# The running row maximum of a graph-attention layer, stored grouped by remainder of four

## The reference, cut to what matters

```
scores = einsum('hbnd,hbdm->hbnm', f_self, f_other)
masked = a * scores ; masked = where(masked >= 0, masked, 0.2 * masked) / 4
attn = softmax(masked - 1e9 * (a == 0), axis=-1) ; zero where a == 0
out = relu(attn @ feats + bias)
```

## Time and profile before

| | |
|---|---|
| median of 3 runs | 1647.0 us (1645.42 to 1648.21) |
| span of the profiled execution, first to last instruction | 1639.9 us |
| time of the runs outside that span (median less span) | 7.1 us |
| busy: TensorE / VectorE / ScalarE / GpSimd | 87% / 81% / 76% / 66% |
| mean granted TensorE clock | 0.947 |

### The profile page before, as it was taken

The page is one execution under the profiler, slowest core; times in us unless marked ns, Lnnn a source line. Parts: engine busy times, 40 slices in busy tenths (PEclk is TensorE's granted clock), DMA queues, the critical chain, the costliest instruction groups (busy, mean ns, idle before and its releaser), DMA issues.

```text
span 1639.9 us, 22202 instructions
## 1 busy us (share of the span) xinstructions
PE 1428.8 (87%) x7728; PEld 705.3 (43%) x7728; DVE 1329.8 (81%) x1657; ACT 1243.4 (76%) x1475; POOL 1077.2 (66%) x575
## 2 busy tenths in 40 slices
PE   5897879998998899998889998988899889899766
PEld 3443434444444444444444444444444444345323
DVE  2887878888887888888888788888888788988865
ACT  2697878787887879877787778878788787887731
POOL 3367767766777666677676667777677766767422
PEclk9999999999999999999999999999999999999867
DMA  6523251313423053121513234131342304100000
GB/s 101 69 41 45 46 67 33 46 31 55 55 51 44 20 72 54 42 32 40 78 27 50 25 60 62 37 43 29 55 55 51 44 21 62 39 13 14 26 10 10
DMA packets 57277, 72.02 MB, mean 44 GB/s; under 512 B 23878, under 2 KB 44878, under 8 KB 57166
## 3 DMA queue, kind: packets, MB, share of 16 engines
q0 software_dynamic: 13824, 18.01, 14.6%
q1 hardware_dynamic: 42142, 51.97, 12.9%
q10 hardware_dynamic: 1200, 0.63, 0.2%
HBM read 102.87 MB, written 3.26 MB: 65 GB/s over the span
## 4 chain that ended last, share of the span: by engine, by line
PE 48%; DVE 23%; ACT 12%; issue 11%; DMA 2%; POOL 1%; SPq 1%; ACTq 1%; DVEq 0%; POOLq 0%
PE M L612 11%; DVE RUN L855 10%; PE M L561 9%; PE Z L522 9%; PE Z L524 8%; ACT LS L703 6%; ACT LS L711 3%; PE Z L535 3%; DVE LS L869 3%; PE Z L622 3%; PE Z L683 2%; PE Z L570 1%; DVE X L960 1%; DVE RUN L852 1%; DVE RSTD L948 1%
## 5 line engine op out<-in xcount | busy, mean ns | idle before, releaser
L429 POOL TENSOR_TENSOR LS<-LS,MB 125x1000 f32<-125x1000 f32 x372 | 861.3, 2332 | 413.2 <-DVE LS L869 322.4
L855 DVE TENSOR_TENSOR RUN<-Z,RUN 125x1000 f32<-125x1000 f32 x528 | 631.5, 1196 | 197.5 <-ACT LS L703 186.5
L703 ACT ACTIVATE LS<-Z 125x1000 f32<-125x1000 f32 x576 | 575.2, 999 | 196.9 <-PE Z L524 195.6
L711 ACT ACTIVATE LS<-LS 125x1000 f32<-125x1000 f32 x576 | 595.1, 1034 | 45.5 <-POOL LS L429 24.3
L522 PE MATMUL Z<-AT,BI 126*125 126x500 fp8e4 x1152 | 377.1, 409 | 99.0 <-DVE RUN L855 85.9
L561 PE MATMUL M<-LS,V 125*18 125x500 f32 x2304 | 317.3, 624 | 43.4 <-ACT LS L711 42.6
L524 PE MATMUL Z<-FS,FO 96*125 96x500 bf16 x1152 | 354.7, 390 | 0.0
L869 DVE TENSOR_TENSOR LS<-LS,MB 125x1000 f32<-125x1000 f32 x204 | 286.9, 1411 | 8.2 <-DMA MB<-row_maxima 1.7
L522 PEld LDWEIGHTS Z<-AT,BI 126*125 126x125 bf16 x1152 | 136.1, 141 | 242.6 <-DVE RUN L855 154.2
L524 PEld LDWEIGHTS Z<-FS,FO 96*125 96x125 bf16 x1152 | 162.3, 141 | 107.4 <-issue 14.2
L612 PE MATMUL M<-AT,XP 125*128 125x500 fp8e4 x756 | 203.3, 391 | 0.0
(11 more groups left out here) (120 smaller groups left out, 1003.7 us busy)
## 6 DMA issues: line engine op xcount, KB each, us to landing
MB<-row_maxima SPq DMA_DIRECT2D x48, 500.0 KB, 3.8
A<-in_adj_dram POOLq DMA_DIRECT2D x96, 183.1 KB, 4.8
FO<-PARTS SPq DMA_DIRECT2D x192, 46.9 KB, 2.1
FS<-PARTS SPq DMA_DIRECT2D x180, 46.9 KB, 2.1
XP<-in_x_dram SPq DMA_DIRECT2D x8, 336.0 KB
XA<-in_x_dram SPq DMA_DIRECT2D x8, 336.0 KB
out_dram<-X SPq DMA_DIRECT2D x7, 375.0 KB
row_maxima<-LMAX SPq DMA_DIRECT2D x48, 3.5 KB
```

What stands on the lines that cost most here:

```text
L429: nc.gpsimd.tensor_tensor(rows, rows, MB[:P, u % 2, :, :], ALU.subtract).then_inc(sub_pool, 1)
L703: nc.scalar.activation(LS[:P, q % RL, :, :], banks("Z", q)[:P], ACT.Prelu, alpha=0.2).then_inc(bent, 1)
L711: nc.scalar.activation(rows, rows, ACT.Exp, scale=0.25).then_inc(exps, 1)
L855: nc.vector.tensor_tensor(run, z, run, ALU.max).then_inc(maxed, 1)
```

## The change

RUN keeps its place and its size, but within each head its 500 columns are stored as four runs of 125: column 4i + c of the scores lies at place 125c + i. The transposes read 125 neighbouring columns where they read every fourth. VectorE walks Z in the old order (i outside, c inside), and writes RUN, and in line 855 reads it too, at steps of 125 float32 (500 bytes), going back by 374 after every fourth. Reductions, transfers, semaphores and the order of every queue are the same.

```diff
@@ turn_run
-  last = nc.tensor.transpose(z[:P, hh, c * P:(c + 1) * P], RUN[:, u % 2, hh, c:C:ST], ID[:P, :P])
+  last = nc.tensor.transpose(z[:P, hh, c * P:(c + 1) * P], RUN[:, u % 2, hh, c * P:(c + 1) * P], ID[:P, :P])
@@ maximum
-  run, z = RUN[:, u % 2, :, :], banks("Z", q)[:P]
+  run = RUN[:, u % 2, :, :].rearrange("p h (c i) -> p h i c", c=ST)
+  z = banks("Z", q)[:P].rearrange("p h (i c) -> p h i c", c=ST)
```

## The result

The changed kernel takes 1865.0 us (1864.2 to 1866.4) against 1647.6 us before: a ratio of 1.132, with a 95% interval of 1.130 to 1.134. It is slower by 13%, inside the forecast range and by the forecast mechanism; the predicted 1970 us were 105 too many.

What follows compares the result with a forecast made beforehand. No single engine bound the kernel before; afterwards VectorE would bound the maxima stage. 1254.6 us busy plus 518 added gives 1773, plus 50 idle, 140 outside the stage and 7 for the median: 1970 us, range 1780 to 2190.

Steps and rivals of the forecast that it cites:

- What bounds: In the maxima stage, engines nearly equally loaded; VectorE has 245 us idle to absorb the change, 0.43 us per instruction.
- What it removes: Line 535's transposes: load 323 to 189 ns, eight in 1.03 us instead of 2.09; 0 to 51 us gained, nearest 25.
- the second rival: VectorE's hops in RUN cost nothing and TensorE's transposes halve: kernel faster, 1622 us, 1596 at best; chance 0.09.
- What it adds: VectorE's 576 maximum instructions on RUN, lines 852 and 855, take 0.90 us more each through 500-byte hops.
- the load's ratio of 1.85: Line 535's stepped weight load takes 1.85 times as long per column; carried to VectorE, 0.90 us more per instruction.
- three readings of the load's row: Line 535's load carried to VectorE's maximum by ratio (0.90 us more), by difference (1.07) or by pace (1.28).
- The memset row: Line 841's VectorE memset at steps of 18 float32, 138 ns for 96: a stepped write costs nothing, the lower end.
- The sum: Whole kernel: 518 us added makes VectorE the stage's bound; 1773 busy, 50 idle, 140 elsewhere: 1963 us, with 7 more 1970.
- The ring: TensorE, ScalarE and VectorE pass three bank pairs round; 64 steps leave VectorE 0.8 us idle each, about 50 us.
- The 7 us on top: Whole kernel: the measured median of 1647.0 us stands 7 us above the profiled span of 1639.9, added to the forecast.
- The heavier hop: In line 855 read and write penalties add up, 1.8 us more each: about 2490 us; chance 0.07 for above 2190.
- the light one: VectorE's hops cost 0.05 to 0.55 us an instruction, mostly taken by idle time: 1730 us; chance 0.05 for 1650 to 1780.

Runs made afterwards that it cites:

- run with every second unit: RUN stored by remainder for odd units only, in maximum and transposes, the other units as in the kernel before: 1753.6 us, ratio 1.064.
- VectorE's part alone: The changed kernel's maximum combined with the transposes of the kernel before, which read every fourth column: 1866.3 us, ratio 1.132 to the kernel before.

## Why the prediction was right, and where its sum was off

**What bounds.** This was right. Neither engine was the bound before; the 245 us that VectorE had to spare were outrun by the added work, and the stage took VectorE's pace. The run with every second unit adds that idle time left in one unit does not help the next.

**What it removes.** The load (199 ns for about 190) and the eight transposes (1.14 us for about 1.05) were right within 10%, and that TensorE's saving vanishes was shown by VectorE's part alone. The 25 us that the second rival took for TensorE's gain were mis-sized: 11 were measured.

**What it adds.** This was right in kind and mis-sized: 0.75 us an instruction instead of 0.90. The step that was off is the load's ratio of 1.85 carried over to VectorE; VectorE's own is (1927 - 142)/1054 = 1.69 for a read hop and 1.72 for both. Of the three readings of the load's row the ratio was still the nearest. The memset row misled as a lower end: line 853 only writes, and pays 0.74 us. Of the figures in the Trainium skill's page "Vector Engine (DVE) Microarchitecture Reference", section "Measured stream behaviour on trn2", the trace agrees within 5% with the hopping write (1.71 ns an element there, (1928 - 142)/1000 = 1.79 here) and with one hopping source (1.73 there, 1.79 here). Its 1.98 is for all three ports hopping; here Z does not hop, and one source and the write together take 1.81. Its need for neighbouring pairs does not hold for a step of two words, which took 1.06 ns here.

**The sum.** The stage's forecast was 1773 us busy and 50 idle; it came out as 1632 and 92. The busy part is 141 too high: 576 x 0.15 = 85 by the hop's price; 41 because line 870's subtracts became shorter (286.9 us before, 245.8 after), which I had not foreseen; and about 15 because VectorE's instructions overlap more, one starting up to 0.1 us ahead of the end of the one before. Their durations in the stage add up to some 73 us more than VectorE's busy time before, and to 90 in the changed kernel.

The idle part is 42 too low. Line 856's wait for the bend is the 50.9 us that I expected, but in part by luck: 27 us of it lie where I had it, in 39 maxima that follow a step with two more entries, and 24 us in 38 other places. The ring has 55 such steps, not 64, since not every graph has all eight, and they cost 0.5 us each, not 0.8. What I left out is 37 us of gaps under 0.15 us between VectorE's instructions, 23 of them ahead of line 856. 1963 - 141 + 42 is the span of 1864. The 7 us on top were mostly spread between runs: the profiled execution took 1865.7 us for its 1863.9.

**The rivals.** The heavier hop falls (the ports overlap), the free one and the light one fall (0.75 us), and the transposes did gain. TensorE's granted clock fell in the stage from 0.96 to 0.90, and line 522's matmul rose from 409 to 440 ns. VectorE's wait for the bend came out at 50.9 us all the same, so the 40 us that the range kept for this were not needed.

## What to carry to other kernels

Price an access pattern by what two elements in a row share. In VectorE's maxima and TensorE's loads, float32 steps of 8 bytes were free, and steps of 16 bytes (on VectorE also of 500) added 0.6 to 0.7 of the instruction's time, while in VectorE's maxima one neighbour in each run made hops of 1000 and 2000 bytes free. A memset is no guide to that price: the one of the earlier trace rows paid nothing at a step of 72 bytes. Before moving a stride from one engine to another, count how often each walks the data: here 48 turns paid for the stride before and 576 maxima after. And when a stride seems to be a mere cost, look for what it buys elsewhere; here it was the run of four numbers in a transfer that GpSimd's subtracts wait for.

## What the runs showed of the hardware that was not expected

VectorE's subtract, with both operands in SBUF, seems to wait for GpSimd's two-operand instructions. These are the subtracts of the kernel before and of the changed one, with shortest, median and longest ns:

```profile
L869 DVE TENSOR_TENSOR LS<-LS,MB x204: 1186/1192/3309, 76.9 to 1571.9; 125x1000 f32<-125x1000 f32 x102
```

```profile
L870 DVE TENSOR_TENSOR LS<-LS,MB x204: 1167/1198/2204, 89.2 to 1794.7; 125x1000 f32<-125x1000 f32 x102
```

One of the long ones in the timeline of the kernel before:

```profile
1145.47 4.59 POOL L429 TENSOR_TENSOR LS<-LS,MB 125x1000 f32<-125x1000 f32 x2
...
1147.87 3.25 DVE L869 TENSOR_TENSOR LS<-LS,MB 125x1000 f32<-125x1000 f32 x1
```

GpSimd ends at 1150.06, and the subtract 1.06 us later, as if its elements had only then begun to flow (1000 elements at VectorE's 1.054 ns). Of the 204 subtracts, the 61 that overlap a GpSimd tensor instruction take 1.92 us on average, the other 143 take 1.19 and none over 1.20. In the changed kernel GpSimd waits for VectorE longer (484.6 us in all, 322.4 before), only 37 of 204 overlap, at 1.27 us, and VectorE gets 41 us back. Which of the two began first seems to matter: there the 15 that began during a GpSimd instruction take 1.38 us, the 22 that began ahead of one 1.20. No run took the overlap away by itself, so this is read from the traces and not tried.
